# Cross-attention block: stacked low halves of the context products, two buffers of exponentials, one load of small vectors, and a new instruction order

## What is computed

```
# first layer
xn = layernorm(x, ln1_w, ln1_b);  yn = layernorm(ctx, ln2_w, ln2_b)
q = xn @ Wq;  k, v = split(yn @ Wkv)              # 256 -> 256, 192 -> 512
o = softmax(q k^T / 4) v                          # per head
x = x + o @ Wproj + bproj
x = x + gelu(layernorm(x, ln3_w, ln3_b) @ W1 + b1) @ W2 + b2      # 256 -> 1024 -> 256
# second layer
xr = x * rsqrt(mean(x^2) + eps) * norm_w
q = unit(rotate(xr @ wq));  k, v = split(ctx @ wkv);  k = unit(rotate(k))
out = x + (softmax(4 q k^T) v) @ wout
```

## Time and profile before

| what | value |
|---|---|
| median of 3 runs | 375.3 us (374.32 to 375.59) |
| profiled execution, its own time | 370.83 us |
| its span, first to last instruction | 368.9 us |
| mean granted TensorE clock | 0.991 |
| busy: PE, PE's weight loads | 339.2 us (92%), 299.6 us (81%) |
| busy: DVE, ACT, POOL | 268.2 us (73%), 220.8 us (60%), 189.0 us (51%) |
| moved by DMA | 12.45 MB |

### The profile page before, as it was taken

The page is one execution under the profiler, slowest core; times in us unless marked ns, Lnnn a source line. Parts: engine busy times, 40 slices in busy tenths (PEclk is TensorE's granted clock), DMA queues, the critical chain, the costliest instruction groups (busy, mean ns, idle before and its releaser), DMA issues.

```text
span 368.9 us, 9747 instructions
## 1 busy us (share of the span) xinstructions
PE 339.2 (92%) x3832; PEld 299.6 (81%) x3832; DVE 268.2 (73%) x594; ACT 220.8 (60%) x395; POOL 189.0 (51%) x163
## 2 busy tenths in 40 slices
PE   5888878999989999999999999989999999999985
PEld 5576666878767787899999999989998888877764
DVE  6877999899998658946769988577535777436433
ACT  1457364556555565485755656637477877677761
POOL 3174996532435020452198999949664938605000
PEclk9699999999999999999999999999999999999999
DMA  7707510010001000000000000000000000000001
GB/s 182 238 3 218 148 45 10 8 46 0 4 2 44 24 2 2 23 2 3 0 23 3 0 23 24 0 6 19 2 0 2 2 16 31 31 16 30 30 31 59
DMA packets 14910, 12.45 MB, mean 34 GB/s; under 512 B 3985, under 2 KB 14225, under 8 KB 14865
## 3 DMA queue, kind: packets, MB, share of 16 engines
q1 hardware_dynamic: 13376, 11.17, 10.3%
q10 hardware_dynamic: 1488, 0.66, 0.7%
HBM read 9.73 MB, written 2.10 MB: 32 GB/s over the span
## 4 chain that ended last, share of the span: by engine, by line
PE 60%; DVE 13%; POOL 10%; issue 7%; ACT 5%; DMA 3%; ACTq 1%; SPq 0%; DVEq 0%; POOLq 0%
PE bank_y L1031 8%; PE bank_o L1031 7%; PE banks_s L1206 7%; POOL norm_k_inv L408 5%; PE banks_s L1272 4%; DVE row_max L2083 4%; PE banks_s L1122 4%; ACT PT L655 3%; PE banks_s L1106 2%; PE bank_o L1217 2%; PE bank_o L1153 2%; PE bank_t L1031 2%; POOL norm_q_inv L420 2%; PE bank_qk L1031 2%; PE bank_y L1217 2%
## 5 line engine op out<-in xcount | busy, mean ns | idle before, releaser
L420 POOL TENSOR_TENSOR norm_q_inv<-norm_q_min,minus_half 128x32 f32<-128x32 f32 x8 | 45.3, 5665 | 21.7 <-DVE norm_q_min L2265 21.7
L408 POOL TENSOR_TENSOR norm_k_inv<-norm_k_min,minus_half 128x32 f32<-128x32 f32 x8 | 45.1, 5636 | 11.6 <-DVE norm_k_min L2233 11.6
L635 ACT ACTIVATE PT<-banks_s 128x1024 f32<-128x1024 f32 x32 | 31.0, 1023 | 22.1 <-PE banks_s L1131 22.1
L2083 DVE TENSOR_REDUCE row_max<-banks_s 128x8 f32<-128x1024 f32 x32 | 37.5, 1214 | 3.3 <-PE banks_s L1106 3.1
L666 ACT ACTIVATE W_s<-banks_s,b_cols 128x256 f32<-128x256 f32 x62 | 25.9, 470 | 17.7 <-PE banks_s L1206 17.6
L1206 PE MATMUL banks_s<-lnT_hi,W_hi 128*128 128x256 f32 x124 | 35.6, 287 | 0.0
L655 ACT ACTIVATE PT<-banks_s 128x1024 f32<-128x1024 f32 x32 | 31.0, 1023 | 6.7 <-PE banks_s L1272 6.6
L1206 PE MATMUL banks_s<-lnT_lo,W_hi 128*128 128x256 f32 x124 | 35.0, 283 | 0.0
L1206 PE MATMUL banks_s<-lnT_hi,W_lo 128*128 128x256 f32 x124 | 35.0, 282 | 0.0
L372 POOL TENSOR_TENSOR x_all<-x_all,b_row 128x256 f32<-128x256 f32 x16 | 13.2, 842 | 32.8 <-DVE b_xn L2166 32.8
L675 ACT ACTIVATE hT_hi<-W_s 128x512 fp32r<-128x512 f32 x32 | 20.2, 632 | 13.7 <-PE bank_o L1217 5.3
(11 more groups left out here) (326 smaller groups left out, 1039.2 us busy)
## 6 DMA issues: line engine op xcount, KB each, us to landing
x_all<-in_x SPq DMA_DIRECT2D x16, 128.0 KB, 3.0
W_s<-in_L_xattn_W SPq DMA_DIRECT2D x2, 1024.0 KB, 7.0
out<-x_all SPq DMA_DIRECT2D x16, 128.0 KB, 1.7
ctx_in<-in_ctx SPq DMA_DIRECT2D x16, 96.0 KB, 3.5
ctx_in<-in_ctx_T SPq DMA_DIRECT2D x8, 128.0 KB, 2.3
ctx_in<-in_ctx_T SPq DMA_DIRECT2D x8, 64.0 KB, 2.5
W_s<-in_L_xattn_Wq ACTq DMA_DIRECT2D x1, 256.0 KB, 3.4
W_s<-in_L_xattn_Wkv ACTq DMA_DIRECT2D x1, 256.0 KB, 3.9
```

The costliest lines, as they stand in the source:

```text
L408: nc.gpsimd.tensor_tensor(norm_k_inv[:, :], norm_k_min[:, :], minus_half[:, :], ALU.pow).then_inc(c_kinv, 1)
L420: nc.gpsimd.tensor_tensor(norm_q_inv[:, :], norm_q_min[:, :], minus_half[:, :], ALU.pow).then_inc(c_qinv, 1)
L635: nc.scalar.activation(PT[:, 2 * h:2 * h + 2, :], banks_s[:, 2 * h:2 * h + 2, :], ACT.Exp, scale=HD ** -0.5)\
L2083: v.tensor_reduce(row_max[:, 8 * h:8 * h + 8], banks_s[:, 2 * h:2 * h + 2, :].rearrange("p n (r k) -> p (n r) k", k=TOK), AX.X, ALU.max).t ...
```

## The change

- The context is loaded 256 columns wide, its last 64 columns twice (`ctx_wide`, and `ctx_T` with 256 rows). `Wkv_r` and `wkv_r` hold in the second half of depth the high part in rows 0 to 63 and the low part in rows 64 to 127, so that `stacked_mm` needs five products for six: 10 for 12 in `keys_a`, `values_mm_a`, `keys_c` and `values_mm`. On DVE `stack_wkv` makes the low rows; POOL's `split_wkv` has six steps for eight.
- The bias of keys is now added by ACT (two operations for one in `keys_out_a`), that of values is folded into the projection's (`values_bias`, `proj_bias`, `proj_bias_out`); `kv_bias` is 16 products of one column for 4 of 512.
- `PT` has two buffers, and `exps_a` and `exps_c` wait for the weighted product of one tile earlier.
- Eight loads of small vectors and two of masks become one (`small_t`), the first on ACT's queue.
- `x` and context of tiles 4 to 7 are loaded ahead of `W2`, not only 4 and 5.
- The memsets of banks and pads on DVE go; idle turns on PE stand in four groups of 16, 10, 4 and 8 for one of 28.
- The order of the calls on POOL, ACT, PE and DVE is another one throughout.

The core of the diff:

```diff
-WARM = 28
+WARM = 10
...
-        PT = sb("PT", 128, NG, 512)
+        PT = sb("PT", 128, 2, NG, 512)
...
-                sp.dma_start(ctx_in[:, t % AHEAD, 0:C2], ctx[bass.ds(t, 1)]...)
+                sp.dma_start(ctx_in[:, t % AHEAD, :], ctx_wide[bass.ds(t, 1)]...)
...
-            for t in range(AHEAD, AHEAD + 2):
+            for t in range(AHEAD, 2 * AHEAD):
                 load_x(t)
                 load_ctx(t)
...
+            act.dma_start(small_t[:, :], small).then_inc(small_loaded, LOADED)
             act.dma_start(Wq_s, Wq.rearrange("(t p) n -> p t n", p=128)).then_inc(wq_loaded, LOADED)
             act.dma_start(Wkv_s[:, 0, :], Wkv[0:128, :]).then_inc(wkv_loaded, LOADED)
-            act.dma_start(Wkv_s[0:C2B, 1, :], Wkv[128:C2, :]).then_inc(wkv_loaded, LOADED)
-            for n, v in enumerate((ln1_w, ln1_b)):
-                act.dma_start(ln1_cols[:, n, :], ...).then_inc(ln_loaded, LOADED)
-            for n, v in enumerate((ln2_w, ln2_b)):
-                act.dma_start(ln2_cols[:, n, 0:1], ...).then_inc(ln_loaded, LOADED)
-                act.dma_start(ln2_cols[0:C2B, n, 1:2], ...).then_inc(ln_loaded, LOADED)
+            for half in (slice(0, C2B), slice(C2B, 128)):
+                act.dma_start(Wkv_s[half, 1, :], Wkv[128:C2, :]).then_inc(wkv_loaded, LOADED)
...
             def exps_c(t):
                 act.wait_ge(c_scores, t + 1)
-                act.wait_ge(av, NB + t)
+                act.wait_ge(av, NB + t - 1)
...
+            def stacked_mm(out, a, b, data):
+                for n, (x, y) in enumerate(HI_LO):
+                    mm(out, a[:, x, 0, :], b[:, y, 0, :], start=n == 0, stop=False)
+                for x in range(2):
+                    last = mm(out, a[:, x if data == 0 else 0, 1, :], b[:, x if data else 0, 1, :], start=False, stop=x == 1)
+                return last
...
             def keys_c(p, bank):
...
-                    last = split_mm(bank[:, in_pair(j, C1)], ctxT_r[:, :, :, in_pair(j, TOK)], wkv_r[:, :, :, 0:C1])
+                    last = stacked_mm(bank[:, in_pair(j, C1)], ctxT_r[:, :, :, in_pair(j, TOK)], wkv_r[:, :, :, 0:C1], 0)
```

More of the change, by code:

```diff
@@ L59, in wait, with build @@
         eng.wait_ge(sem, count)
-def build(nc, x, ctx, ln1_w, ln1_b, ln2_w, ln2_b, ln3_w, ln3_b, Wq, Wkv, Wproj, bproj, W1, b1, W2, b2,
-          norm_w, wq, wkv, wout, ctx_T, rope, halves, picks, out):
+def build(nc, x, ln3_w, ln3_b, Wq, Wkv, Wproj, bproj, W1, W2, b2, wq, wkv, wout, ctx_wide, ctx_T, rope, small, out):
     es = ExitStack()
@@ L602, in queries_out_a @@
                 for m in range(KT):
-                    last = nc.scalar.activation(qkT[:, p % 2, m, :], bank[:, in_pair(m, 2 * TOK)], ACT.Identity, bias=bq_cols[:, m:m + 1])
+                    last = nc.scalar.activation(qkT[:, p % 2, m, :], bank[:, in_pair(m, 2 * TOK)], ACT.Identity, bias=bias_cols[:, m:m + 1])
                 last.then_inc(a_q, 1)
@@ L609, in keys_out_a @@
                 wait(act, a_shifted, 2 * p - 2)
-                nc.scalar.activation(qkT[:, p % 2, KT:, :], joined(bank[:, :]), ACT.Copy).then_inc(a_k, 1)
+                if p == 0:
+                    act.wait_ge(a_bkv, 1)
+                for m in range(KT):
+                    last = nc.scalar.activation(qkT[:, p % 2, KT + m, :], bank[:, in_pair(m, 2 * TOK)], ACT.Identity, bias=bias_cols[:, KT + m:KT + m + 1])
+                last.then_inc(a_k, 1)
             def values_out_a(p, bank):
@@ L1905, in _ @@
-            inputs_c(7, bank_o)
+            pe.wait_ge(c_qrope, 16)
+            project(20, bank_o)
+            pe.wait_ge(c_masked, 12)
+            normed(21, bank_y)
+            pe.wait_ge(on_ready, 22)
+            back(22, bank_t)
+            pe.wait_ge(res_ready, 21)
+            weighted(23, bank_o)
+            pe.wait_ge(c_exped, 18)
+            scores_c(9)
+            pe.wait_ge(onT_lo, 22)
+            queries_T(6, bank_y)
+            pe.wait_ge(oT_ready, 24)
+            project(21, bank_o)
@@ L2361, in _ @@
[L2361 removed]
+            maxima_rows(8, bank_y)
             normalise(12)
             normalise(13)
[L2364 to L2374 removed]
+            residual(5, bank_y)
@@ new lines, in _ @@
+            heads_out(6, bank_o)
+            maxima(9)
+            out_lo(6, bank_o)
+            maxima_parts(9)
+            rows_lo(6, bank_y)
+            statistics(14)
+            heads_out(7, bank_o)
+            normalise(14)
+            maxima_rows(9, bank_y)
+            context_lo_a(6, bank_t)
+            maxima(10)
+            residual(6, bank_y)
+            maxima_parts(10)
+            out_lo(7, bank_t)
+            heads_out(8, bank_o)
+            maxima_rows(10, bank_y)
@@ new lines, in _ @@
+            statistics(15)
+            stack_wkv(0)
+            residual(7, bank_o)
+            normalise(15)
+            maxima(11)
+            out_lo(8, bank_o)
+            rows_lo(7, bank_t)
+            weights_c(1)
+            heads_out(9, bank_o)
+            maxima_parts(11)
+            weights_c(2)
+            maxima_rows(11, bank_o)
+            maxima(12)
+            residual(8, bank_o)
+            maxima_parts(12)
+            out_lo(9, bank_qk)
+            context_lo_a(7, bank_y)
```

2067 lines of the change are left out of this document (1014 added, 1053 removed).

## The result

The changed kernel takes 354.0 us (median of 4 runs, 353.5 to 354.6) where the kernel before takes 374.8 (median of 4, 370.3 to 375.6): ratio 0.947, 95% interval 0.939 to 0.955, 5% faster. The forecast was 354. That it came out to the microsecond is luck, two errors that cancel: the span is 5.0 us longer than the sum had it (352.8 for 347.8), and the 4.5 us that I added between the time of a profiled execution and the median do not exist for this kernel (its profiled execution took 354.6, the median is 354.0).

The account below looks back on a forecast made before the run. PE was taken to bound the kernel everywhere, with both windows of a first-attention tile overfilled. Stretch by stretch the span fell 21.1 us, 368.9 to 347.8; 370.8 became 349.7, plus 4.5 to the median 354.2, given as 354, range 346 to 366.

Parts of the forecast that it names:

- second attention: First to last scores there: 70 us (67 to 76) against 80.9, with the weighted product under the next tile's exponentials.
- window sum: Second attention: the new order's periods added up by PE's prices, 67.6 us, before room was left for ACT and DVE.
- first rival: Both attentions: DVE and ACT hold the tile, period stays 8.3 (+6.0), second attention never below 4.3 (+5.6): 365.8; chance 0.12.
- From the last scores to the end the chain is as before: 12.2: End of the kernel: the time from the last scores to the end stays 12.2 us.
- First attention, 12 x 7.8: First attention after its first three periods: twelve tile periods of 7.8 us (7.5 to 8.3), where 8.29 was measured.
- For the first three periods I take 21 us: First attention's first three periods: 21 us, windows nearly empty; W2's later load ends a wait of 5.33 us.
- The start: Before the first scores: they move from 22.9 to 18.9 us, 4.0 earlier (2.5 to 5.5).
- Saturated stretch: Between the attentions: 132.1 us (130 to 137) for 128.6, -3.0 from fewer products, +6.5 from work brought forward.
- in the saturated stretch it pays in full: Between the attentions: ten products for twelve save their whole PE time, 12 groups losing 0.25 us each (-3.0).
- I keep that distance: Whole kernel: the median stays 4.5 us above the profiled execution's time, so 349.7 becomes 354.2.
- POOL's inverse roots: Slower rival: PE waits at turns behind roots of 5.6 us each; four uncovered (22.4) cancel the gain, worst 388; chance 0.03.
- The fitting order: Rival: no misfit in either attention, 12 x 0.3 and 2.4 us less: 348.2; chance 0.10.

Follow-up runs that it names:

- experiment 1: Kernel after with one buffer of exponentials again, and out_hi(20) ahead of the exponentials of tile 7 on ACT: 388.0 us.
- experiment 2: Kernel before with two buffers of exponentials and nothing else: 374.75 us, ratio 1.0004.
- experiment 11: Kernel after with POOL's w2_lo later, 18 idle turns in a PE gap, W1's load later, tile 11's DVE work and the last tiles reordered: 347.3 us.
- experiment 5: Kernel after with POOL's four w2_lo parts moved behind residual_bias(9), DVE's order unchanged: 352.7 us for 354.0.
- experiment 6: Kernel after with DVE reordered around tile 11: statistics(15) and normalise(15) earlier, weights_c(1) behind maxima_parts(11): 356.2 us.
- experiment 9: Kernel after with 18 turns of the unit matrix filling PE's wait before rows_T(2): 352.6 us for 354.0.
- experiment 3: Kernel after with one more matmul in each of the 64 context products, so 12 for 10 again: 359.8 us.
- experiment 4: Kernel before, in its old order, with 10 matmuls for 12 in each context product: 370.7 us, ratio 0.9875.

## Why the prediction was right

The number was right by luck in its last microseconds, the mechanism in its main part. The largest term is the second attention, 13.5 of the 20.8 us, against 1.7 more in the stretch to which some of its work was moved, and there both the mechanism and the size held. The terms named as failed or mis-sized below were not right.

*Second attention: right.* Two buffers and the new order took the window sum, 67.6, nearly to the letter: 67.4. The 70 that I took for want of room on ACT and DVE was too careful. Tail 3.64 for 3.7. Experiments 1 and 2 show that neither half does it alone. (The first rival's +5.6 for this stretch is 5.2 by the prediction's own list of periods.)

*"From the last scores to the end the chain is as before: 12.2": failed.* 14.7. The delay that gains in every period costs one at the end: a tile more of weighted product, turns and projection lies behind the last scores. Experiment 11 got 2.0 of it back.

*First attention, 12 x 7.8: mis-sized, 8.1.* The steady periods were right. The two bad ones are 5.5 us over the 7.8, the other ten together 2.0 under it: that makes the 3.6 us. DVE's weight work (`weights_c`, the stacking) was priced at a size but never at a place: beside POOL. For tile 4 experiment 5 shows this cause. For tile 11 it is shown in part only: the collision of `normalise(15)` with POOL's masks is in the trace (1.13 us for 0.41 each), but experiment 6 lost time and experiment 11, with another order, had 0.9 us back. The trace of the kernel before had the sign, and the prediction did not use it. One and the same instruction, line and shape, takes 400 to 1399 ns there, and the longest stands beside POOL's work on `W_lo`:

```profile
L2064 DVE TENSOR_SCALAR xn<-x_all,mean_var,rstd x16: 400/419/1399, 10.6 to 106.3; 128x256 f32<-128x256 f32 x16
...
50.63 1.27 POOL L353 TENSOR_TENSOR W_lo<-W_s,W_hi 128x512 fp32r<-128x512 f32 x1
50.66 1.40 DVE L2064 TENSOR_SCALAR xn<-x_all,mean_var,rstd 128x256 f32<-128x256 f32 x1
```

*"For the first three periods I take 21 us": 23.5.* The wait on W2's load went, as said, but a 2.5 us wait for normalised rows was left, with a halved clock behind it (0.5 to 2.4 us by experiment 9 and the traces without its turns).

*The start: 19.7 for 18.9.* One of its terms failed and one held: Wkv's last piece was there at 8.7 and not at 7.3; the clock did fall to 0.50 from 12 to 14 us in spite of the idle turns, yet was up again for the first queries (1.68 us at 14.30). The forecast for the clock in "What would show it", 1.00 from 12 to 18 us, failed with that. The new start as a whole is worth more than the 4.0, 5.5 on the mean: the old one varies, 22.9, 24.8, 26.7, 28.9 in four traces of the old loads, the new one 19.0 to 21.4 in nine. In the four old ones the last small load lands at 9.2, 9.6, 11.1 and 12.1, and the clock is back at 1.00 at 18.7, 21.5, 23.1 and 25.8. So the landing moves by 2.9 us and the first scores by 6.0; how much of the gain is due to the loads and how much to the clock was not separated.

*Saturated stretch: 130.3 for 132.1.* Busy time grew by 2.9 us (126.34 to 129.20; summed: 3.5) and idle time fell from 2.3 to 1.1. The step that failed is "in the saturated stretch it pays in full": by experiments 3 and 4 idle time takes up 0.6 to 1.7 us of 2.5 to 2.7.

*"I keep that distance": failed.* In every execution here time and span differ by 1.8 to 2.6 us. The 4.5 us between 370.8 and 375.3 were not outside the span: the profiled execution had an early start and one fall of the clock fewer. That spread belongs to the old kernel's start and waits. The fall from 374.8 to 354.0 is 20.8 us beside the 21.1 of the sum, but by another way: the kernel before has a span of some 372.9 on the median (374.8 less 1.9) and not 368.9, the kernel after 352.2 and not 347.8. Both ends lie some 4 us higher than the sum had them.

*The rivals.* DVE and ACT do not hold the tile at 8.3: ten of twelve periods are shorter. POOL's inverse roots never showed in PE's waits. The fitting order was near in the second attention alone.

## What to carry to other kernels

An order made from measured durations has to know which durations hold only while a neighbour is quiet. The sign in a trace is one line and shape with very different durations. Where such work meets GpSimd's on the way that PE waits for, as `weights_c(0)` did, move one of the two, and look what it meets at its new place. Price a wait of PE like those of 1.6 to 2.9 us here at its length and at what may follow at half clock; idle turns in it may save the second part, as in experiment 9. Before one profiled execution is made the base of a sum, compare its time with the other runs: this one lay 4 us below the median. Where work is put one tile later to hide a step, count the extra tile at the end, and give the last tiles their own order and spare buffers.

## What was not expected of the hardware

- A VectorE instruction of 0.17 us (the cast of 16 columns) took 1.03 us beside GpSimd's work. It loses 0.86 us, about as much as an instruction of twice its length (0.35 us, which took 1.12).
- The same wait of 1.6 us left the clock at 1.00 in one execution and took it to 0.50 in another. In these two executions that is 1.2 us of 3.2; the other 2.0 are in the start. The kernel before spreads from 370.3 to 377.1 us from run to run, the kernel of experiment 11 from 346.7 to 348.3.
- Eight small loads for one, 3.4 us more of issues ahead of the weights, moved the first scores by 9.9 us, from 19.7 to 29.6 (8.2 to 10.7 against the nine traces with this start).
